# Gated delta rule layer: taps read from PSUM, the Gram tile loaded back, and other orders

## The reference

```
q, k, v = silu(conv4(x @ Wq.T)), silu(conv4(x @ Wk.T)), silu(conv4(x @ Wv.T))
q, k = l2_norm(q), l2_norm(k)
alpha = exp(-exp(A_log) * softplus(x @ Wa.T + dt_bias)); beta = 2 * sigmoid(x @ Wb.T)
S = alpha * (S - beta * k (k^T S)) + k v^T        # token after token
o = rms_norm(S^T q) @ Wo.T
x = x + layernorm(o)
```

## Time and profile before

| | |
|---|---|
| median of three runs | 3788.26 us (3783.3 to 3788.53) |
| profiled execution, its own time | 3825.41 us |
| its span | 3823.6 us |
| TensorE matmuls busy | 2960.6 us, 77% |
| VectorE busy | 2599.0 us, 68% |
| ScalarE busy | 2461.6 us, 64% |
| GpSimd busy | 2038.0 us, 53% |
| mean granted TensorE clock | 0.891 |

### The profile page before, as it was taken

The page is one execution under the profiler, slowest core; times in us unless marked ns, Lnnn a source line. Parts: engine busy times, 40 slices in busy tenths (PEclk is TensorE's granted clock), DMA queues, the critical chain, the costliest instruction groups (busy, mean ns, idle before and its releaser), DMA issues. The chain is left out here.

```text
span 3823.6 us, 187747 instructions
## 1 busy us (share of the span) xinstructions
PE 2960.6 (77%) x79010; PEld 2359.3 (62%) x79010; DVE 2599.0 (68%) x4634; ACT 2461.6 (64%) x3772; POOL 2038.0 (53%) x2143
## 2 busy tenths in 40 slices
PE   5588887878787877787778788777787878787665
PEld 4366666666666666666666666666666666666533
DVE  5577776767677766676667677666776767776453
ACT  2566666666666666666667666666666667676543
POOL 1356655555555565555555555555555555555335
PEclk9789988999898989898988988989998988889877
DMA  2343433343333334333433343334333433343211
GB/s 64 68 80 71 78 58 76 73 77 58 74 75 76 63 69 80 71 66 66 80 71 67 65 80 71 69 62 79 72 67 64 79 72 67 65 80 71 46 34 44
DMA packets 888600, 262.88 MB, mean 69 GB/s; under 512 B 812992, under 2 KB 862400, under 8 KB 887872
## 3 DMA queue, kind: packets, MB, share of 16 engines
q1 hardware_dynamic: 887584, 250.08, 34.8%
q0 software_dynamic: 288, 1.07, 0.1%
HBM read 177.63 MB, written 56.64 MB: 61 GB/s over the span
## 5 line engine op out<-in xcount | busy, mean ns | idle before, releaser
L872 DVE SCALAR_TENSOR_TENSOR cv<-raw,w_v,cv 128x1024 f32<-128x1024 f32 x384 | 631.6, 1645 | 4.6
L1088 POOL TENSOR_TENSOR accT<-accT,yt 128x512 f32 (+1 forms) x256 | 367.8, 1437 | 462.3 <-DVE yt L1001 459.9
L872 DVE SCALAR_TENSOR_TENSOR cv<-raw,w_kq,cv 128x1024 f32<-128x1024 f32 x384 | 553.9, 1443 | 21.6 <-ACT cv L720 19.3
L982 DVE SCALAR_TENSOR_TENSOR R<-ps,sc,R 128x128 f32<-128x128 f32 x1024 | 281.7, 343 | 318.3 <-PE ps L622 315.6
L712 ACT ACTIVATE raw<-ps 128x1024 f32<-128x1024 f32 x256 | 264.7, 1034 | 277.3 <-PE ps L500 277.3
L973 DVE COPY Z<-ps 16x128 f32<-16x128 f32 x512 | 146.9, 287 | 384.3 <-PE ps L603 378.9
L1075 POOL TENSOR_TENSOR Sg<-S,tabR 128x512 f32<-128x512 f32 x256 | 307.8, 1202 | 164.4 <-DVE S L991 164.4
L1042 POOL TENSOR_TENSOR QG<-sl_q,QG 128x1024 f32<-128x1024 f32 x64 | 166.0, 2594 | 391.5 <-DMA QG<-scrG 391.5
L1009 POOL TENSOR_TENSOR raw<-raw,k_all 128x24 f32<-128x24 f32 x256 | 241.4, 947 | 194.2 <-DVE cv L872 115.2
L576 PE MATMUL ps<-Z,Nd 64*64 64x64 f32 x8192 | 204.1, 242 | 172.9 <-DMA Z<-scrZ 164.5
L500 PE MATMUL ps<-xnT,w_kq 128*128 (+1 forms) x512 | 322.1, 785 | 13.4 <-DMA w_kq<-wtab 13.4
(11 more groups left out here) (198 smaller groups left out, 7687.1 us busy)
## 6 DMA issues: line engine op xcount, KB each, us to landing
E<-scrE SPq DMA_DIRECT2D x128, 256.0 KB, 4.7
scrN<-Nd SPq DMA_DIRECT2D x256, 128.0 KB
Z<-scrZ SPq DMA_DIRECT2D x128, 256.0 KB, 5.6
X<-scrX SPq DMA_DIRECT2D x512, 64.0 KB
QG<-scrG SPq DMA_DIRECT2D x128, 256.0 KB, 4.1
kB<-sk SPq DMA_DIRECT2D x64, 256.0 KB
w_kq<-wtab SPq DMA_DIRECT2D x64, 132.0 KB, 3.4
w_v<-wtab SPq DMA_DIRECT2D x64, 132.0 KB, 3.1
```

The costliest lines, as they stand in the source:

```text
L872: nc.vector.scalar_tensor_tensor(cv3[j], raw3[j][:, :, k:k + P], tap(j, k), cv3[j], ALU.mult, ALU.add).then_inc(conv[j].sem, 1)
L982: last = nc.vector.scalar_tensor_tensor(unit(R, b), ps[:, col128(PB["ks"][s], g, i)], cr[:, 8 * s + b:8 * s + b + 1], unit(R, b), ALU.mult ...
L1088: nc.gpsimd.tensor_tensor(dst, dst, row(half(yt, h)), ALU.add).then_inc(acc_ok[h][s].sem, 1)
```

## The change

- Taps from PSUM: `act_raw`, `pool_tail`, the tile raw, its memset and the constants for its tails are gone. `pe_proj` now handles one chunk at a time, with the three columns ahead of it (67 columns for each batch), so four projections of two matmuls become eight. `act_tap0` and `dve_conv` read the projection in PSUM, half a chunk pair (512 elements) at a time.
- Gram tile loaded back: a new tile NM gets the whole of Nd back from scrN (`sp_nm`), and `pe_y` multiplies NM where it multiplied Nd. `pool_eb` no longer waits for `pe_y` of the pair before, and `sp_gram` waits for the load.
- `act_yr` scales wo's product out of PSUM on ScalarE, in four instructions of 128 columns; `dve_yr` is left uncalled. `act_z0` takes the place of `dve_z0`. `pool_sq_k` takes the place of `act_sq_k`.
- All five body lists are in another order, PB has other banks, and the waits for banks follow from both.

```diff
-RAW = NB * (P + HALO)
+CW = C + HALO
...
-        raw = sb("raw", 4 * RAW)
+        NM = sb("NM", 1024)
...
-                nc.gpsimd.memset(raw[:], 0.0).then_inc(zeroed.sem, 1)
...
-        PB = {"Pk": 0, "Pq": 4, "Pv": 0, "Pw": 4, "nk": 4, "nq": 6, "gk": [4, 0], "gp": [4, 2], "ktr": [6, 4], "vt": [2, 4], "y0": [0, 2], "z0": [0, 6], "y1": [6, 6], "xt": [0, 4], "z1": [6, 0], "ks": [2, 2], "u": [2, 2], "ds": [2, 6], "o": [6, 6], "ms": [6, 4], "wo": [0, 2]}
+        PB = {"Pk": [4, 2], "Pq": [0, 0], "Pv": [4, 0], "Pw": [2, 0], "nk": 0, "nq": 0, "gk": [2, 4], "gp": [2, 2], "ktr": [2, 0], "vt": [6, 0], "y0": [6, 0], "z0": [6, 2], "y1": [6, 0], "xt": [2, 2], "z1": [6, 6], "ks": [4, 6], "u": [6, 6], "ds": [6, 6], "o": [4, 4], "ms": [4, 2], "wo": [6, 0]}
...
+        def pj(j, s):
+
+            return bank(PB["P" + "kqvw"[j]][s], 2).rearrange("p (b t) -> p b t", b=NB)
...
-                last = nc.tensor.matmul(bank(PB["P" + "kqvw"[j]] + g), w[:, (j % 2) * P:(j % 2 + 1) * P],
-                                        xnV[:, 4 * g:4 * g + 4, bass.ds((p % 8) * P, P)], start=True, stop=True)
+                last = nc.tensor.matmul(pj(j, s)[:, 4 * g:4 * g + 4, 0:CW], w[:, (j % 2) * P:(j % 2 + 1) * P],
+                                        xnT3[:, 4 * g:4 * g + 4, bass.ds((p % 8) * P + s * C, CW)], start=True, stop=True)
...
-                pe.wait_ge(nd_ok[s].sem, nd_ok[s].at(p))
+                pe.wait_ge(nm_in.sem, nm_in.at(p))
...
-            nc.scalar.activation(cv3[j], raw3[j][:, :, 0:P], ACT.Copy, scale=tap(j, 0)).then_inc(tap0[j].sem, 1)
+            nc.scalar.activation(cv3[j][:, :, s * C:(s + 1) * C], pj(j, s)[:, :, 0:C], ACT.Copy, scale=tap(j, 0)).then_inc(tap0[j][s].sem, 1)
...
+        def act_yr(act, p, s, h):
+            act.wait_ge(wo_mm[h][s].sem, wo_mm[h][s].at(p))
+            act.wait_ge(rt_ok.sem, rt_ok.at(p + 1))
...
+            for i in range(4):
+                f = 8 * s + 4 * h + i
+                last = nc.scalar.activation(half(yt, h)[:, i * D:(i + 1) * D], ps[:, col128(PB["wo"][s], h, i)], ACT.Copy,
+                                            scale=ro[:, f:f + 1])
...
-            nc.vector.scalar_tensor_tensor(cv3[j], raw3[j][:, :, k:k + P], tap(j, k), cv3[j],
-                                           ALU.mult, ALU.add).then_inc(conv[j].sem, 1)
+            c = cv3[j][:, :, s * C:(s + 1) * C]
+            nc.vector.scalar_tensor_tensor(c, pj(j, s)[:, :, k:k + C], tap(j, k), c, ALU.mult, ALU.add).then_inc(conv[j][s].sem, 1)
...
+        def pool_sq_k(pool, p):
...
+            nc.gpsimd.tensor_tensor(sq[:], sk[:], sk[:], ALU.mult).then_inc(sq_k.sem, 1)
...
+        def sp_nm(sp, p):
+            if not first(p):
+                sp.wait_ge(y_mm[1][B].sem, y_mm[1][B].at(p - 1))
+            sp.sem_inc(sp_go.sem, 1)
+            sp.wait_ge(n_out.sem, n_out.at(p))
+            for h, (a, z) in enumerate(HALF):
+                sp.dma_start(NM[a:z].rearrange("p (n t) -> p n t", t=C), rows(scrN, h)).then_inc(nm_in.sem, 16)
```

More of the change, by code:

```diff
@@ L821, in act_x, with act_z0 @@
             nc.scalar.activation(two(X[:]), quads(PB["xt"][s]), ACT.Copy).then_inc(x_ok[s].sem, 1)
+        def act_z0(act, p, s):
+            act.wait_ge(z_mm[0][s].sem, z_mm[0][s].at(p))
+            zp = quads(PB["z0"][s]).rearrange("p g (b c) -> p g b c", b=4)
+            zs = two(half(Z, s)).rearrange("p g (b c) -> p g b c", b=4)
+            for r in range(0, P, 32):
+                o = r % C
+                last = nc.scalar.activation(zs[r:r + 16, :, :, o + 16:o + 32], zp[r:r + 16, :, :, o + 16:o + 32], ACT.Copy)
+            last.then_inc(z_ok[0][s].sem, 1)
         def act_z1(act, p, s):
@@ new lines, in pe_body @@
+            if p1 is not None:
+                pe.wait_ge(conv[2][A].sem, conv[2][A].at(p1))
+                pe_gram_k(pe, p1, B)
+            if p3 is not None:
+                if p2 is not None:
+                    pe.wait_ge(y_ok[0][B].sem, y_ok[0][B].at(p2))
+                elif p1 is not None:
+                    pe.wait_ge(n2_ok.sem, n2_ok.at(p1))
+                elif p3 is not None:
+                    pass
+                pe_wo(pe, p3, B, 0)
+            if p2 is not None:
+                if p1 is not None:
+                    pe.wait_ge(nd_ok[A].sem, nd_ok[A].at(p1))
@@ new lines, in act_body @@
+            if p1 is not None:
+                act_abs(act, p1)
+                act_tap0(act, p1, A, 2)
+            if p2 is not None:
+                act_z1(act, p2, A)
+            act.preload_act_table_set("natural_log_exp_and_others")
+            if p1 is not None:
+                act_exp(act, p1)
+            if p2 is not None:
+                act_u(act, p2, A, 0)
+                act_y(act, p2, B, 0)
+            act.preload_act_table_set("silu_and_others")
+            if p1 is not None:
+                act_silu_q(act, p1)
@@ L1600, in act_body @@
+            if p2 is not None:
+                act_u(act, p2, A, 1)
+                act_v(act, p2, B, 1)
+            if p3 is not None:
+                act_yr(act, p3, B, 0)
+            if p2 is not None:
+                act_z0(act, p2, B)
+            if p3 is not None:
+                act_yr(act, p3, B, 1)
+            if p2 is not None:
                 act_v(act, p2, B, 0)
+                act_x(act, p2, B)
+                act_oc(act, p2, A)
+                act_y(act, p2, B, 1)
             if p1 is not None:
-                act_tap0(act, p1, 3)
+                act_tap0(act, p1, A, 3)
@@ L1635, in act_body @@
             if p1 is not None:
+                act_xb(act, p1)
+            act.preload_act_table_set("silu_and_others")
+            if p1 is not None:
+                act_silu_v(act, p1, 0)
+            if p2 is not None:
+                act_oc(act, p2, B)
+            if p1 is not None:
+                act_silu_v(act, p1, 1)
+            if p2 is not None:
+                act_yr(act, p2, A, 0)
+            if p0 is not None:
+                act_tap0(act, p0, A, 0)
+            if p2 is not None:
+                act_yr(act, p2, A, 1)
+            if p0 is not None:
+                act_tap0(act, p0, A, 1)
+            if p1 is not None:
                 act_v(act, p1, A, 0)
```

707 lines of the change are left out of this document (253 added, 454 removed).

## The result

The changed kernel takes 3987.95 us (median of four runs, 3972 to 3996) against 3787.52 for the kernel before in the same measurement: a ratio of 1.0526, 95% interval 1.0488 to 1.0564. It is slower by 200 us. I had forecast 3550, and the range ended at 3780.

The account below looks back on a forecast made before the run. Bound: a circuit through several queues, about 54 us per pair. New links sum to 48.9 us, with stalls 50.3, 3.75 less; over 64 pairs 240 us, with the memset 243: 3788 - 243, rounded to 3550 us, range 3390 to 3780.

Parts of the forecast that it names:

- to y, by Z or by ScalarE: From substitution to y: Z back, or ScalarE's copy XB, silu, yr, first taps and v's pieces; both 10.6 us.
- y to the end of the body: y, query norms, z, keys times state, R, last projection, evictions and semaphores: 7.4 us.
- jump: TensorE's gap at the jump back to the top of the body, 3.54 us, 3.9 with its block.
- z, Gram, key norms: TensorE's first blocks in the body, four blocks' worth at half clock: 3.7 us.
- to the state's change: TensorE's small blocks, u, ds and wo at full clock, 8.2 us, plus ScalarE's evictions in between, 0.7.
- S, keys times state, R, taps: Before the substitution: adding S 1.3 us, keys times state 1.0, R 2.2, six taps 4.7, two tiny ones 0.6.
- allowed for stalls: Stalls "issue" inside the body, on top of 48.9 us: 1.4 us each at the transposes of keys, bounds 0 to 3.
- Half speed behind the jump: After the jump's gap TensorE is granted 0.50, 1.2 GHz: blocks of 32 small products count 0.9 us, not 0.5.
- Taps: VectorE's 24 taps from PSUM at 742 ns: 18.7 us per pair against 18.5, 0 in sum, between -2.0 and +1.7.
- The Gram tile's load at nothing: Two more 256 KB issues on SP, about 2 us, hidden in its 16.7 us wait; without that cover, +2.
- The slower rival: ScalarE's waits stay, 17.5 us without work: period 55.6 us, 3890 us in all; decided above 16 us; chance 0.16.
- Banks held until the third tap: PSUM banks of projections, formerly freed at once by a copy, might hold TensorE up for 2 us: 52.3 per pair, 3675.

Follow-up runs that it names:

- with 104 increments: The change with 104 empty semaphore increments on TensorE ahead of the loop, nothing else different: 3612.14 us, ratio 0.954 to the kernel before.
- written out: Every engine's hardware loop written out, so no jumps: the change 3521.49 us (0.9329), the kernel before 3649.9 (0.9676).
- with 168 increments: The change with 168 empty semaphore increments on TensorE ahead of the loop: 3664.14 us, ratio 0.9698 to the kernel before.
- with 40: The change with 40 empty semaphore increments on TensorE ahead of the loop: 3822.8 us, ratio 1.0101 to the kernel before.

## Why the prediction was wrong, by its own steps

One repetition of the change, stage by stage against the sum. The ends are read from the timelines: substitution 2000.64 to 2004.94, y starts 2017.10, last projection ends 2026.41, z starts 2029.52, key norms end 2035.85, the change of the state 2046.17, next substitution 2056.74.

| stage | sum said | measured | difference |
|---|---|---|---|
| substitution | 4.6 | 4.30 | -0.3 |
| to y, by Z or by ScalarE | 10.6 | 12.16 | +1.6 |
| y to the end of the body | 7.4 | 9.31 | +1.9 |
| jump | 3.9 | 3.11 | -0.8 |
| z, Gram, key norms | 3.7 | 6.33 | +2.6 |
| to the state's change | 8.9 | 10.32 | +1.4 |
| S, keys times state, R, taps | 9.8 | 10.57 | +0.8 |
| sum | 48.9 | 56.10 | +7.2 |
| allowed for stalls | 1.4 | in the above | -1.4 |

5.8 us per pair too little in this repetition, 6.5 by the mean of 56.8: 64 of these are 416 us, and 3550 + 416 = 3966 beside 3988. (54.0 less 50.3 is 3.7, where the prediction has 3.75; that is 3 us in all.) The stops inside the body, jump aside, are 2.52 + 2.27 + 0.51 + 0.54 = 5.8 us of the +7.2; the other terms together were short by 1.4.

**The step that failed** is the last of the sum, "On top come stalls 'issue' inside the body ... 1.4 us each", with its bounds of 0 to 3. I took the price from one line of the kernel before, though its table of waits had others like it:

```profile
PE ps L511 <- issue: 78.1, 49, 4.0
...
PE ps L643 <- issue: 59.3, 58, 1.8
PE ps L603 <- issue: 41.5, 72, 1.9
```

Less the jump the waits "issue" of the kernel before are 292 us, 4.6 per pair, over the upper bound of 3 already. And I treated the stop as a property of a kernel, like a duration, where it is a property of where the loop lies. Per pair, and without the jump, the waits "issue" are 6.9 us in the change ((588 - 148) / 64, 148 being 57 jumps at 2.6) and 2.6 with 104 increments ((333 - 165) / 64), for the same instructions. The period with 104 is 50.8 us, where the sum had 50.3. That is the rest of the circuit borne out, and some luck as well: 104 was one of four placements, and its 2.6 us of stops are over the 1.4 allowed. I had read the gap at the jump as a thing by itself, and not seen that "issue" at the jump, at the transposes of keys and elsewhere was one cause with a spacing that can be counted. The list of orders even showed what matters: behind the jump before stood keys times state, a few projections; in the change the blocks of 32 and 64 small products. What was missing was a count of TensorE's instructions from the loop's start.

**The circuit was right in its links, not in every length.** The way by v's R ends last at y (the wait of 1.37), 1.6 us later than I counted, because ScalarE starts late on it:

```profile
2003.00 1.02 ACT L862 ACTIVATE osq<-ps 128x1024 f32<-128x1024 f32 x1 [3.09 <-PE ps L643]
...
2006.54 0.64 ACT L881 ACTIVATE XB<-XT 128x256 f32<-128x256 f32 x1
```

It waited 3.09 us for the second chunk's output, and the row of small work behind that ran past the substitution's end at 2004.94. The copy XB came 1.6 us after it. The sum let ScalarE be free. Z, which I had meeting it within 0.1 us, had landed at 2014.9, 2.2 us ahead of y. Whether ScalarE's own list or the transposes of v (from 2013.70, R from 2014.50) held R up, no run separates; taking wo's pieces off ScalarE gained nothing clear.

**Clock.** Half speed behind the jump came true, but it lies later than I had it. In the change it begins inside the second stop, at 2030.5, and ends at 2037.3. By windows of 1 us:

```profile
2033.00:2034.00 1.00, 1.00 (x48) 1.00 (x45) 0.00 (x0) 0.66 (x2) 0.00 (x0) 0.50 0.07 16
2034.00:2035.00 1.00, 1.00 (x48) 1.00 (x44) 0.00 (x0) 0.98 (x2) 0.00 (x0) 0.50 0.00 0
2035.00:2036.00 1.00, 1.00 (x37) 1.00 (x33) 0.00 (x0) 0.99 (x2) 0.00 (x0) 0.50 0.00 0
2036.00:2037.00 1.00, 1.00 (x16) 1.00 (x14) 0.56 (x4) 0.46 (x1) 0.00 (x0) 0.50 0.00 0
```

It is granted 0.50, the 1.2 GHz level, on past the key norms into u, which the sum had at full clock; that and the stop of 0.51 are in the +1.4, and I have not split them. With 104 increments half speed lasts as long, from 2045.6 to 2052.5, but z has run by then, at 0.69 us and full clock; the key norms ran at half.

**Taps** were right, in their duration; no run tests their effect on the time. The groups of single lines, the tap and the parts that ScalarE took over (ns min/median/max):

```profile
L891 DVE SCALAR_TENSOR_TENSOR cv<-ps,w_kq,cv x768: 741/750/753, 106.5 to 3688.2; 128x512 f32<-128x512 f32 x192
...
L873 ACT ACTIVATE yt<-ps,sc x1024: 359/386/431, 193.2 to 3772.5; 128x128 f32<-128x128 f32 x171
...
L825 ACT ACTIVATE Z<-ps x512: 251/269/272, 153.0 to 3746.2; 16x128 f32<-16x128 f32 x171
```

750 ns where 742 was worked out, and none of 768 over 753, where those from SBUF went up to 3389. 24 x 0.75 = 18.0 us stand against 18.5 before. The estimate by the Trainium skill's page "VectorE: DVE Perf Modes", section on the TRN2 errata, 632 cycles or 658 ns, is 12% too low, and a loss of 2.3 us per pair by it did not come. What the Trainium skill's page "GPSIMD Engine Reference", section "Specifications", says of contention with two inputs in SBUF fits that no tap from PSUM was long. wo's pieces cost 0.386 each, 16 of them 6.2 us of pure duration; in a row they overlap, four in 1.13 or 1.18.

**The Gram tile's load at nothing**, "hidden in the 16.7 us that SP waits", was the second wrong step. SP was indeed not held up; its wait for the inversion fell to 2 us per pair and others took its place, without a lost microsecond on scrZ, issued 0.02 us after the substitution's end:

```profile
SPq L1143 <- PE ps L640: 392.8, 63, 9.8
...
SPq L1180 <- DVE XT L981: 127.3, 63, 8.3
```

What it costs lies on another resource, the DMA engines that carry the instructions: some 31 to 44 us written out, GpSimd's copy in its place included, and nothing that shows in the change as made. A doubled load costs far more.

**The slower rival** had the right sign and the wrong cause. ScalarE is without work for 17.4 us of the 56.1, past the 16 from which that case was to decide. But nothing about ScalarE's list differs in the change with 104 increments, and that is 376 us faster; ScalarE is without work for 12.2 us of its 50.8 there, and for 18.3 of 56.8 in the change (means over 600 to 3300 us). Some 6 us of this idle time come and go with the placement alone: they are a result of the stops, not their reason. Banks held until the third tap never showed: over the whole span of the change taps ended two waits of projections, 5.6 us together.

## What to carry to other kernels

Before pricing an edit to a kernel whose loop is dense with small instructions, find the waits "issue", count the instructions between two of them, and see into which product each boundary falls and how many instructions stand behind the jump; then compare versions at several placements, or written out, since placement alone moved this kernel by 376 us and the edits moved it by 128. If a boundary must fall somewhere, a place behind a few long instructions looks best: the kernel before had eight projections of 5.4 us there and no stop. That is read from one placement and not tested by itself. A load whose landing ends no wait still takes the DMA engines on which the next instructions come.

## What the runs showed of the hardware that I had not expected

- TensorE's instructions come in blocks of 256, one packet of 0.02 MB each (164635 instructions, 643 packets, written out). Stops stand at multiples of 123 to 124 matmuls with their weight loads and are up to 4.0 us long; some boundaries show none. Empty semaphore increments ahead of the loop shift them one for one, to within three matmuls.
- A jump back costs TensorE 2.6 to 3.7 us in the median of each looped run read here, and if the next boundary comes 14 to 17 matmuls later, another 1.7 to 2.5. With 57 to 120 matmuls between them the second stop was 0.85 to 1.2.
- The same loop body took 3612, 3664, 3823 or 3988 us by its place alone, and the kernel before 3788, 3904 or 3982.
- TensorE went on 2.3 to 2.9 us after the start of the packet with its instructions, in the median at each place where it stopped, on idle DMA engines and on busy ones. At the jump with 168 increments it was 3.5. What the busy ones added was mostly the time until the packet started, about 2 us.
- Doubling a load of 512 KB per pair, whose landing ended no wait of TensorE, cost 137 us written out and 252 us looped.
- What is left open: why the stop in mid body of the change (2.27 us at line 600) shrinks to 0.56 with 104 increments but to only 1.81 with 40. Its boundary lies in another product each time, and I did not vary that alone; nor did I find the best number of increments.
